# A mixture-of-experts layer whose first twelve expert tiles run off a list made before attention has ended

## The chip, the cores and the metric

The kernel runs on one core of a Trainium2 chip, as one launch. The metric is the device time in microseconds (us), the median of three runs. TensorE (PE in the profile) does matmuls, VectorE (DVE), ScalarE (ACT) and GpSimd (POOL) work on tiles in SBUF and PSUM, SyncE (SP) issues DMAs, and GpSimd issues those with indices (indirect DMAs).

## The reference

Eight sequences of 512 tokens with 512 features pass through cross-attention (16 heads) and a mixture of experts, each with a layer norm ahead and a residual around it. All is float32.

```python
x = x + attention(layernorm(x), ctx, ctx)          # B=8, S=512, D=512, 16 heads of 32
flat = layernorm(x).reshape(4096, 512)
scores = softmax(flat @ router_weight.T + router_bias)   # E=8 experts
topk_vals, topk_idx = top_k(scores, 2)
w = zeros.at[arange[:, None], topk_idx].set(topk_vals)
gu = einsum('th,ehf->tef', flat, gate_up_proj) + gate_up_bias
gate = minimum(gu[..., :512], 7.0); up = clip(gu[..., 512:], -7.0, 7.0)
act = (up + 1.0) * gate * sigmoid(gate * 1.702)
down = einsum('tei,eih->teh', act, down_proj) + down_bias
x = x + einsum('teh,te->th', down, w)
```

## The kernel before

It has three stages, each a block of its own: a block's engines meet at its end (a DRAIN on each, and an exchange of semaphores) before the next block begins. Lines 1129, 1363 and 1799 are the ends of attention_stage, routing_stage and expert_stage.

**Attention** runs over 32 units (a batch b and a chunk c of four heads). The function step(s) lists what is done while unit s takes its exponentials, in eight rounds; all engines walk the one list ORDER and do their own part of it. A unit's output projection, residual, second layer norm and router logits follow some steps later, a tile of 128 tokens at a time (keys "norm", "out", "x2", "rstd", "ln2", "turn_xln", "logits", "logit_sum", "logit_out"). x2 and the normed rows (xln_dram) go to memory. Routing goes along by groups of tiles (route_groups): "best" finds the two experts of each token, "count" keeps running counts, "rank" gives each token its place within its expert by two matmuls, "place" makes the positions, and "list" writes token numbers by indirect DMAs of GpSimd into token_list, which has 32 rows of 128 places for each expert. "soft" and "share" make the weights of the two experts. The last group has five tiles.

**Routing** (routing_stage) makes the counts into whole tiles of 256 tokens for each expert: 39 tiles, with tile_expert, tile_changed (does the tile need other weights than the tile two before), tile_hot and token_of (the token of each place). The last group's tokens are put in by matmuls of one-hot rows (at_hot, col_hot), the others by reading token_list back.

**Experts** (expert_stage) runs over the 39 tiles. in_list takes even tiles from the first half of the list and odd ones from the second, so there are two sets of weights in SBUF, and each is loaded only if the expert changed. All products are in three passes of a high and a low part (fp32r), so that a weight needs, after its DMA into raw_g or raw_d, wg_hi or wd_hi (ScalarE) and wg_lo or wd_lo (VectorE, gate_up_lo and down_lo). For a tile i TensorE transposes the gathered rows (turn_rows), does gate/up in four parts f (96 matmuls of 256 columns, L1489) and down (24 of 512 columns, L1503); it works in the order turn_rows(i+2), gate_up(i+1), down(i). VectorE does in each part: clip (L1612, L1614), glu (L1619, L1622), hidden_lo (L1627), between them xgT_lo of the next rows (row_lo), the pieces of the next weights, and at f = 1 the mix (L1645, L1648), which adds the down result of tile i-1 to the gathered sums. down(i) waits for that mix, since d_ps has one bank for each half. GpSimd gathers rows (L1733) and sums (L1745) and scatters sums (L1750); SyncE loads weights and biases behind two register loads each.

```python
load_if_changed(e, tile_expert, tile_changed, tile, semaphore, experts, copies)   # SyncE: two value_loads, a conditional DMA
with e.If_ne(changed, 0):
    gu_lo(e, s, k)
with e.Else():
    e.sem_inc(wg_lo_made[s], 1)
```

Of the kernel before, what the change touches and what calls it, by code (L numbers as in the profile page):

```python
# [14 lines left out]
P = 128  # L15
# [8 lines left out]
PASSES = ((0, 0), (0, 1), (1, 0))  # L24

# [12 lines left out]
def list_tile(e, token_list, listed, pos, token, n):  # L38

    places = token_list.rearrange("r (q a) -> (r q) a", a=1)  # L40
    for s in range(TOP_K):
        at = bass.IndirectOffsetOnAxis(ap=pos[:, s, n:n + 1].bitcast(U32), axis=0)
        e.indirect_dma_start(out=places, out_offset=at, in_=token[:, n:n + 1], in_offset=None).then_inc(listed, 16)
# [25 lines left out]
def attention_stage(nc, x, ctx_t, w_t, bq, bk, bv, bo, router_wt, router_b, out, xln_dram, w_rows, w_stored, token_list, listed, stored, route, ident):  # L69
# [9 lines left out]
    expo, hots, weight, exp_sum, inv_sum = (route[n] for n in ("expo", "hots", "weight", "exp_sum", "inv_sum"))  # L79

    SLOTS = 2 * T
    GROUPS = route_groups(B * T, T)
    groups = range(len(GROUPS))
    tiles_of = lambda g: slice(GROUPS[g][0], sum(GROUPS[g]))
    slots_of = lambda g: slice(GROUPS[g][0] % SLOTS, GROUPS[g][0] % SLOTS + GROUPS[g][1])

    with ExitStack() as ctx:
# [4 lines left out]
        def begin_at(name, place):  # L92

            gap = (place - nc.sbuf_base) % 128
            if gap:
                ctx.enter_context(nc.sbuf_tensor(f"gap_{name}", [P, gap], mybir.dt.uint8))
# [8 lines left out]
        begin_at("weights", 0)  # L105
        for n in "kv":
# [3 lines left out]
        ctxT, ctx_raw = split("ctxT", [P, C, S])  # L110
        wo = sb("wo", [P, C, D])
        xT = sb("xT", [P, C, S])
# [6 lines left out]
        hi, lo = ({n: sb(f"{n}_{part}", [P, S], F32R) for n in "kq"} for part in ("hi", "lo"))  # L119
        qs = [sb(f"qs{i}", [P, GROUP, S], F32R) for i in range(RING)]  # L120
        ks = [sb(f"ks{i}", [P, GROUP, S], F32R) for i in range(RING)]
# [23 lines left out]
        consts_i = sb("consts_i", [P, route["consts"].shape[1]], I32)  # L145
        tri = sb("tri", [P, P], BF16)
        expert_less = sb("expert_less", [P, E])
        logits = sb("logits", [P, SLOTS, E])
        masked = sb("masked", [P, SLOTS, E])
        best = sb("best", [P, TOP_K, SLOTS])  # L150
        pick = sb("pick", [P, SLOTS])
        pos = sb("pos", [P, TOP_K, GROUPS[-1][0]], I32)
        pos_f = sb("pos_f", [P, TOP_K, SLOTS])

# [19 lines left out]
        def step(s):  # L174
# [49 lines left out]
            for r, lag, *keys in ((1, 9, ("best", 0)), (2, 9, ("best", 1)), (3, 9, ("count",)), (5, 9, ("soft",)),  # L224
                                  (2, 10, ("rank",)), (3, 10, ("place",)), (1, 11, ("share",))):
                g, odd = divmod(s - lag, T)
                if g in groups[:-2] and not odd:
                    at(r, *[(kind, g, *what) for kind, *what in keys])
            g, t = divmod(s - 11, T)
            if g in groups[:-3]:  # L230
                at(3, ("list", g, t))
            if s == units[-1]:
                at(2, ("list", groups[-3], 0))
                at(3, ("list", groups[-3], 1))
            if s == units[-1] + 1:
                at(1, ("list", groups[-3], 2), ("list", groups[-3], 3))
# [27 lines left out]
            if s + 2 in units:  # L264
# [28 lines left out]
                else:  # L293
# [4 lines left out]
                    at(4, ("low", u, "q"), ("v", u, 0))  # L298
# [1606 lines left out]
```

## Time and profile before

| | |
|---|---|
| median of three runs | 1712.31 us (1709.18 to 1713.91) |
| the profiled execution | 1708.13 us |
| its span in the profile | 1706.4 us |
| mean granted TensorE clock | 0.974 |
| TensorE busy | 1588.7 us, 93% of the span |
| VectorE busy | 1268.3 us, 74% |
| ScalarE, GpSimd busy | 656.5 us, 839.8 us |

A window's row gives for each engine the busy microseconds and, in brackets, the instructions. A timeline's row is start, length, engine, line, operation, output and inputs with shapes, how many were merged, and in square brackets the idle time before it with what ended it. In the chain a row is start, length, engine, result and line.

### The profile page before, as it was taken

The page shows a single profiled execution, that of the slowest core. Times are in us where ns is not written, and L with a number is a line of the kernel's source. Part 1 is how long each engine was busy: PE and PEld are TensorE (multiplying, and loading weights), DVE is VectorE, ACT ScalarE, POOL GpSimd, SP SyncE. Part 2 cuts the span into 40 slices and gives each one's busy share as a digit, 9 for nine tenths or more (in the row PEclk, how much of TensorE's full clock was granted, in tenths as well). Part 3 has the DMA queues.
Part 4 walks back from the last instruction along what each step waited for, and adds up shares of the span by engine and source line. Part 5 has one row for each costly group of instructions (what it writes and reads, how often), then busy time and mean ns, then how long its engine had stood idle before and what let it go on. Part 6 is the DMA issues. An engine that isn't in the chain of part 4 may idle for free. (4 is left out here: it accounts for less than half of the span.)

```text
span 1706.4 us, 30244 instructions
## 1 busy us (share of the span) xinstructions
PE 1588.7 (93%) x9612; PEld 1164.9 (68%) x9612; DVE 1268.3 (74%) x2414; ACT 656.5 (38%) x1267; POOL 839.8 (49%) x634
## 2 busy tenths in 40 slices
PE   6898999999999999999998379999999999999995
PEld 4555555565555555655543179999999998999994
DVE  4576777878768778787685668777888788777873
ACT  3254544545445445454443143223333234223320
POOL 3355656566566676666677322333343333333332
PEclk9899999999999999999999779999999999999997
DMA  6343333443443434433321262325443353324321
GB/s 219 82 113 85 107 107 92 120 99 92 108 104 103 103 97 109 109 89 105 102 80 33 65 218 65 99 88 174 162 165 110 97 210 118 107 82 155 107 88 62
DMA packets 101125, 188.99 MB, mean 111 GB/s; under 512 B 28192, under 2 KB 29600, under 8 KB 100960
## 3 DMA queue, kind: packets, MB, share of 16 engines
q1 hardware_dynamic: 79936, 124.25, 26.0%
q0 software_dynamic: 20832, 62.49, 11.6%
q8 instruction: 77, 1.26, 0.4%
q14 instruction: 88, 0.72, 0.2%
q10 hardware_dynamic: 192, 0.26, 0.0%
HBM read 204.32 MB, written 37.51 MB: 142 GB/s over the span
## 5 line engine op out<-in xcount | busy, mean ns | idle before, releaser
L805 DVE TENSOR_REDUCE negmax<-max_ps 128x2 f32<-128x1024 f32 x252 | 306.9, 1218 | 159.3 <-PE max_ps L545 158.5
L674 ACT ACTIVATE pt<-work 128x512 f32<-128x512 f32 x512 | 278.4, 595 | 275.8 <-PE work L557 265.0
L986 POOL TENSOR_TENSOR acc<-acc,pt 128x1024 f32<-128x1024 f32 x128 | 303.4, 2373 | 127.8 <-ACT pt L674 127.7
L1489 PE MATMUL gu_ps<-xgT_hi,wg_hi 128*128 128x256 f32 x1248 | 349.8, 280 | 1.5 <-DVE xgT_lo L1604 1.5
L1489 PE MATMUL gu_ps<-xgT_lo,wg_hi 128*128 128x256 f32 x1248 | 346.4, 278 | 0.0
L1489 PE MATMUL gu_ps<-xgT_hi,wg_lo 128*128 128x256 f32 x1248 | 346.3, 277 | 0.0
L983 POOL TENSOR_TENSOR acc<-pt 128x1024 f32<-128x1024 f32 x64 | 153.3, 2397 | 184.6 <-PE work L577 115.3
L1489 PEld LDWEIGHTS gu_ps<-xgT_hi,wg_hi 128*128 128x128 f32 x1248 | 235.6, 189 | 2.0 <-issue 1.9
L1750 POOL DMA_INDIRECT out<-acc,token_of x78 | 77.0, 987 | 324.6 <-DVE acc L1648 318.6
L1489 PEld LDWEIGHTS gu_ps<-xgT_lo,wg_hi 128*128 128x128 f32 x1248 | 235.8, 189 | 0.1
L1489 PEld LDWEIGHTS gu_ps<-xgT_hi,wg_lo 128*128 128x128 f32 x1248 | 235.5, 189 | 0.0
L545 PE MATMUL max_ps<-ks,qs 96*128 96x512 f32 x504 | 194.2, 467 | 23.4 <-DVE negmax L805 12.9
L1559 ACT ACTIVATE sig<-gate 128x256 f32<-128x256 f32 x156 | 65.1, 418 | 320.4 <-DVE gate L1612 320.4
L557 PE MATMUL work<-qs,ks 98*128 98x512 f32 x512 | 172.2, 413 | 11.0 <-DVE q_lo L792 5.3
L557 PEld LDWEIGHTS work<-qs,ks 98*128 98x128 f32 x512 | 94.5, 190 | 67.6 <-issue 32.0
L545 PEld LDWEIGHTS max_ps<-ks,qs 96*128 96x128 f32 x504 | 85.6, 193 | 78.4 <-issue 50.1
L569 PE MATMUL o_ps<-pt,v 128*32 128x512 f32 x1024 | 136.4, 605 | 2.0 <-ACT pt L674 2.0
L1503 PE MATMUL d_ps<-wd_hi,hid_hi 128*128 128x512 f32 x312 | 124.2, 398 | 10.1 <-DVE acc L1645 9.6
L1745 POOL DMA_INDIRECT acc<-out,token_of x78 | 80.7, 1035 | 103.6 <-DMA out<-acc,token_of 91.2
L507 PE MATMUL work<-xT,wq 128*128 128x512 f32 x256 | 125.0, 611 | 0.9 <-DMA wq<-wq_t 0.9
L1503 PE MATMUL d_ps<-wd_lo,hid_hi 128*128 128x512 f32 x312 | 124.6, 399 | 0.0
L1503 PE MATMUL d_ps<-wd_hi,hid_lo 128*128 128x512 f32 x312 | 124.0, 397 | 0.0
(221 smaller groups left out, 2897.9 us busy)
## 6 DMA issues: line engine op xcount, KB each, us to landing
raw_g<-w_gate_up SPq DMA_DIRECT2D x39, 2048.0 KB
raw_d<-w_down SPq DMA_DIRECT2D x39, 1024.0 KB
qs<-q_hi SPq DMA_DIRECT2D x252, 64.0 KB, 2.0
ks<-k_hi SPq DMA_DIRECT2D x252, 64.0 KB
bd<-b_down SPq DMA_DIRECT2D x39, 256.0 KB
x_in<-x SPq DMA_DIRECT2D x36, 256.0 KB, 3.3
ctxT_raw<-ctx_t SPq DMA_DIRECT2D x32, 256.0 KB, 4.1
xln_dram<-x SPq DMA_DIRECT2D x32, 256.0 KB, 2.3
```

What stands on the lines that cost most here:

```text
L507: ins = e.matmul(to[:, :], wq[:, k, cols], xT[:, k, :], start=(k == 0), stop=(k == C - 1))
L545: ins = e.matmul(pair_of(u, r)[:, j, :], qs[i][0:3 * HD, h, t * P:(t + 1) * P], ks[i][0:3 * HD, h, :], start=True, stop=True)
L557: e.matmul(to[:, :], ks[i][0:3 * HD + 2, h, k * P:(k + 1) * P], qs[i][0:3 * HD + 2, h, :], start=True, stop=True).then_inc(exp_ready.sem, 1)
L569: ins = e.matmul(o_ps[u % 2][HD * h:HD * (h + 1), :], v[:, k, c * P + HD * h:c * P + HD * (h + 1)], pt[k % 2][:, h, :], start=(k == 0), st ...
L674: e.activation(pt[k % 2][:, h, :], in_work("exp", u, k, h)[:, :], ACT.Exp, scale=scale).then_inc(exped.sem, 1)
L805: e.tensor_reduce(negmax[:, u % 2, n:n + 2], pair_of(u, r)[:, :, :], AX.X, ALU.max, negate=True).then_inc(maxed.sem, 1)
L983: e.tensor_tensor(acc[:, heads, :], pt[0][:, heads, :], pt[1][:, heads, :], ALU.add).then_inc(added.sem, 1)
L986: e.tensor_tensor(acc[:, heads, :], acc[:, heads, :], pt[k % 2][:, heads, :], ALU.add).then_inc(added.sem, 1)
L1489: ins = e.matmul(gu_ps[n % GU_BANKS][:, part, :], wg[s][pw][:, k, cols], xgT[s][px][:, k, :], start=(k == 0 and m == 0), stop=(k == KD - 1 ...
L1503: ins = e.matmul(d_ps[j][:, :], hid[s][px][:, k, j * P:(j + 1) * P], wd[s][pw][:, k, :], start=(k == 0 and m == 0), stop=(k == KF - 1 and ...
L1745: e.indirect_dma_start(out=acc[s][:, j, :], out_offset=None, in_=out_rows, in_offset=slot_rows(i, j)).then_inc(acc_in[s], 16)
L1750: e.indirect_dma_start(out=out_rows, out_offset=slot_rows(i, j), in_=acc[i % 2][:, j, :], in_offset=None).then_inc(scattered.sem, 16)
```

## The change

The list of tiles is cut in two. An early list has twelve tiles of 256 places, all of them full, from the tokens of the first five batches; it is made in attention's steps 27 and 28 from the counts so far (whole_tiles, whole_rows), and at steps 31 and 32 SyncE reads the token numbers back (12 loads), loads the first weights, ScalarE and VectorE split tile 0's gate/up weights, and GpSimd gathers the rows of tiles 0 and 1. These buffers stand where attention's weights, context and stacks of keys were. The routing stage as a block is gone. The rest of the tokens go into a main list of 27 tiles. Its routing, for a last group that now has eight tiles, is done within tiles 0 to 10 of the experts: VectorE takes one step of a generator (route) behind each part f, TensorE does its matmuls in tiles 2, 7, 8 and 9. The mix of tile i-1 moves from f = 1 to the head of the tile's loop, ScalarE's down_hi moves behind f = 1. raw_d and wd_lo share a place, so load_down waits for the down matmuls that used it. In attention the low part of q is placed ahead of the norms of round 4. Places in SBUF are set anew so that operands begin at chosen offsets.

```diff
+EARLY = 12
+EARLY_STEPS = (2, 7, 8, 9)
-    return [(n, batch) for n in range(0, last, batch)] + [(last, batch - 1), (last + batch - 1, batch + 1)]
+    return [(n, batch) for n in range(0, last, batch)] + [(last, 2 * batch)]
...
+            if s == EARLY_END + 7:
+                at(2, ("whole_count",))
+                at(3, ("whole_tiles",))
+            if s == EARLY_END + 8:
+                at(3, ("whole_rows",))
+            if s == units[-1]:
+                at(2, ("load_early", "g"), ("whole_tokens",), ("load_early", "d"))
+                at(7, *[("split_early", k) for k in range(C)])
+            if s == units[-1] + 1:
+                at(0, ("load_early", "g1"))
+                at(1, ("token_of",))
+                at(2, ("fetch_early", 0), ("fetch_early", 1))
...
-            g = groups[-2]
-            if s == units[-1] + 1:
-                at(1, ("best", g, 0), ("best", g, 1), ("count", g), ("rank", g))
-                at(2, ("place", g), ("soft", g))
-            if s == units[-1] + 2:
-                at(0, *[("list", g, t) for t in range(GROUPS[g][1])])
-                at(1, ("share", g))
-                at(5, *[(kind, g + 1, *what) for kind, *what in (("best", 0), ("best", 1), ("count",), ("soft",), ("rank",), ("place",))])
+            if s + 2 in units and s >= 0 and c != 2:
+                at(4, ("low", s + 2, "q"))
...
+                    e.wait_ge(rows_made, 1)
+                    e.wait_ge(early["listed"], 16 * TOP_K * EARLY_END)
+                    for i in range(K):
+                        row = e.value_load(early["row"][0:1, i:i + 1], min_val=0, max_val=E * NT - FTOK // P)
+                        e.dma_start(token_in[:, i, :], token_list[bass.ds(row, FTOK // P), :].rearrange("r q -> q r"),
+                                    allow_slow_non_contiguous=True).then_inc(tokens_in, 16)
...
+                elif kind == "fetch_early":
+                    i, = what
+                    if i == 0:
+                        e.wait_ge(early["tokens_made"], 1)
+                        e.wait_ge(w_stored, 16 * (EARLY_G + 1))
+                        for t in range(T):
+                            e.wait_ge(xln_stored[t].sem, xln_stored[t][EARLY_END // T - 1])
+                        e.wait_ge(exp_ready.sem, exp_ready[units[-1], T - 1, GROUP - 1])
+                    fetch_rows(e, early["xg"][i], early["rows"], early["token_of"], in_list(i, K), early["gathered"][i])
...
-def routing_stage(nc, route, stored, w_rows, ...):
...
+            def rank_last():
+                e.wait_ge(before_made, 1)
+                e.matmul(rank_ps, tri[:, :], hots[:, 0:LEFT, :].rearrange("p t e -> p (t e)"), start=True, stop=False)
+                e.matmul(rank_ps, ones_b[:, :], before[:, 0:LEFT, :].rearrange("p t e -> p (t e)"), start=False, stop=True)
+                e.matmul(count_ps, ones_b[:, :], before[:, LEFT, :], start=True, stop=True).then_inc(handed.sem, 1)
+
+            def choose_rows():
+                e.wait_ge(hot_made, TOP_K)
+                late = [(s, t) for s in range(TOP_K) for t in range(LEFT)]
+                for s, t in late:
+                    e.matmul(late_ps, at_hot[:, s, t, :], col_hot[:, s, t, :, :].rearrange("p a n -> p (a n)"), start=((s, t) == late[0]), stop=((s, t) == late[-1]))
...
-                    gate_up(i + 1, range(KF))
+                    gate_up(i + 1, range(KF // 2))
+                    if i + 1 in (LIST_AT, FIRST_AT, RUN_AT):
+                        e.wait_ge(xgT_lo_made.sem, xgT_lo_made[i + 2, 0])
+                    if i + 1 == LIST_AT:
+                        choose_rows()
+                    if i + 1 == FIRST_AT:
+                        send_first()
+                    if i + 1 == RUN_AT:
+                        count_run()
+                    gate_up(i + 1, range(KF // 2, KF))
+                    if i + 1 == RANK_AT:
+                        e.wait_ge(xgT_lo_made.sem, xgT_lo_made[i + 2, 0])
+                        rank_last()
...
-                    down_hi(i + 1, changed_flag(e, i + 1))
...
+                if now == RANK_AT:
+                    soften()
                 for f in range(KF):
                     gate_sigmoid(now, f)
                     if f:
                         hidden_hi(now, f - 1)
+                    if f == 1 and now:
+                        down_hi(now, changed_flag(e, now))
...
+                for s in range(TOP_K):
+                    last()
+                    then(e.tensor_tensor(at_hot[:, s, :, :], iota[:, :].unsqueeze(1).to_broadcast([P, LEFT, P]),
+                                         at_f[:, s, :].unsqueeze(2).to_broadcast([P, LEFT, P]), ALU.is_equal))
+                    yield
...
+            chain = {(0, 0): (best_experts(0), best_experts(1), count_experts()), (RANK_AT, 2): (share(), place_tokens(), main_tiles()),
+                     (LIST_AT, 2): (take_list(),), (FIRST_AT, 2): (take_first(),), (RUN_AT, 2): (take_run(),)}
+            def route(now, f):
+                under_way.extend(chain.get((now, f), ()))
+                if under_way and next(under_way[0], "end") == "end":
+                    under_way.pop(0)
+                    if under_way:
+                        next(under_way[0])
...
+                if i >= 1:
+                    mix(i - 1)
...
-                    if f == 1 and i >= 1:
-                        mix(i - 1)
+                    route(now, f)
+                    if now == RANK_AT - 1 or f == KF - 1 and RANK_AT <= now < LIST_AT:
+                        route(now, None)
...
+                if i == K:
+                    e.wait_ge(tokens_known, 1)
...
+            def load_down(i):
+                s = i % 2
+                if i >= 2:
+                    e.wait_ge(down_made.sem, down_made[i - 2, SUB - 1])
```

## Rows read from the trace of the kernel before

**Rows 1.** Windows: attention, and its end with routing (PE, PEld, DVE, ACT, POOL, PEclk, DMA).

```profile
0.00:905.00 905.00, 854.77 (x4385) 501.20 (x4386) 673.90 (x1062) 420.99 (x778) 564.04 (x363) 0.99 0.40 106
...
961.00:1000.10 39.10, 8.66 (x38) 7.60 (x39) 23.11 (x85) 6.17 (x9) 9.05 (x11) 0.51 0.41 137
```

**Rows 2.** The chain that ended last, from the first gather on.

```profile
996.66 1.98 PE t_ps L1473 x8
...
1000.13 5.46 PE gu_ps L1489 x24
...
1154.53 10.90 PE gu_ps L1489 x96
...
1380.29 5.47 PE gu_ps L1489 x48
...
1437.29 10.89 PE gu_ps L1489 x96
```

**Rows 3.** TensorE's waits, from 1000 us on, then from 60 to 905 us.

```profile
PE d_ps L1503 <- DVE acc L1645: 9.6, 7, 2.8
...
PE work L557 <- DVE q_lo L792: 5.3, 7, 1.0
```

**Rows 4.** Instructions of the block ends L1129 and L1363; DMA from 966 to 974 us.

```profile
L1129 POOLq DRAIN  x1: 18283/18283/18283, 954.8 to 954.8; - x1
...
L1363 POOLq DRAIN  x1: 462/462/462, 973.4 to 973.4; - x1
...
DMA packets 0, 0.00 MB, mean 0 GB/s; under 512 B 0, under 2 KB 0, under 8 KB 0
```

**Rows 5.** Timelines of VectorE, then GpSimd, from 934 to 966 us.

```profile
934.70 2.33 DVE L857 TENSOR_TENSOR ranks<-ranks,expert_less 128x24 f32<-128x24 f32 x1
...
960.75 0.17 DVE L784 TENSOR_TENSOR logits<-work,rb_rows 128x8 f32<-128x8 f32 x1 [1.03 <-PE work L475]
...
965.18 0.20 DVE L900 COPY ranks<-work 128x40 f32<-128x40 f32 x1 [0.41 <-PE work L483]
...
934.63 2.35 POOL L986 TENSOR_TENSOR acc<-acc,pt 128x1024 f32<-128x1024 f32 x1 [5.78 <-ACT pt L674]
...
937.97 1.04 POOL L43 DMA_INDIRECT token_list<-consts,pos  x1 [0.20 <-issue]
...
962.09 0.96 POOL L43 DMA_INDIRECT token_list<-consts,pos  x1 [0.31 <-issue]
```

**Rows 6.** SyncE's timeline: two DMAs, each behind two register loads.

```profile
994.52 0.37 SPq L1376 DMA_DIRECT2D raw_g<-w_gate_up  x1
996.35 0.37 SPq L1376 DMA_DIRECT2D raw_d<-w_down  x1
```

**Rows 7.** VectorE's timeline: the first clip of tiles 0, 1, 2 and 3.

```profile
1007.55 0.48 DVE L1612 TENSOR_SCALAR gate<-gu_ps,bg 128x256 f32<-128x256 f32 x1
...
1023.96 0.48 DVE L1612 TENSOR_SCALAR gate<-gu_ps,bg 128x256 f32<-128x256 f32 x1
...
1038.58 0.48 DVE L1612 TENSOR_SCALAR gate<-gu_ps,bg 128x256 f32<-128x256 f32 x1
...
1053.99 0.48 DVE L1612 TENSOR_SCALAR gate<-gu_ps,bg 128x256 f32<-128x256 f32 x1
```

**Rows 8.** VectorE's timeline: d_lo, a wait for hid_hi, a tile's end without and with weights.

```profile
1030.55 1.28 DVE L1457 TENSOR_TENSOR wd_lo<-raw_d,wd_hi 128x512 fp32r<-128x512 f32 x2
...
1048.30 0.42 DVE L1627 TENSOR_TENSOR hid_lo<-up,hid_hi 128x256 fp32r<-128x256 f32 x1 [0.55 <-ACT hid_hi L1565]
...
1381.58 0.17 DVE L1698 TENSOR_SCALAR bu<-bg 128x4 f32<-128x4 f32 x1 [1.59 <-ACTq L1544]
...
1417.58 2.36 DVE L1454 TENSOR_TENSOR wg_lo<-raw_g,wg_hi 128x1024 fp32r<-128x1024 f32 x2 [1.09 <-ACT wg_hi L1448]
```

**Rows 9.** VectorE's groups by line in the routing stage (busy us, mean ns).

```profile
L1273 DVE TENSOR_TENSOR at_hot<-iota_f,at_f 128x640 f32<-128x640 f32 x2 | 1.6, 822 | 0.0
L1278 DVE TENSOR_TENSOR col_hot<-col_hot,consts 128x390 f32<-128x390 f32 x2 | 1.1, 566 | 0.1
```

More of the change, by code:

```diff
@@ L79, in attention_stage @@
     expo, hots, weight, exp_sum, inv_sum = (route[n] for n in ("expo", "hots", "weight", "exp_sum", "inv_sum"))
+    logits, masked, best, pick, expert_less, tri = (route[n] for n in ("logits", "masked", "best", "pick", "expert_less", "tri"))
     SLOTS = 2 * T
-    GROUPS = route_groups(B * T, T)
+    GROUPS = route_groups(B * T, T)[:-1]
     groups = range(len(GROUPS))
+    EARLY_G = groups[-2]
+    EARLY_END = sum(GROUPS[EARLY_G])
+    K = early["tiles"]
+    NT = B * T
     tiles_of = lambda g: slice(GROUPS[g][0], sum(GROUPS[g]))
@@ L105, in attention_stage @@
         begin_at("weights", 0)
+        first_place = nc.sbuf_base
         for n in "kv":
@@ L1384, in load_down, with place_of @@
[L1384 to L1389 removed]
+def place_of(n_tiles, early, i):
+    K = early["tiles"]
+    return in_list(i, K) if i < K else in_list(i - K, n_tiles - K)
@@ L1399, in expert_stage @@
     tiles = range(n_tiles)
+    K = early["tiles"]
+    MAIN = n_tiles - K
+    SLOTS = MAIN * SUB
+    NT = rows.shape[0] // P
+    LAST = route_groups(NT, batch)[-1]
+    LEFT = LAST[1]
+    weights_stored = len(route_groups(NT, batch))
+    TILE_SHIFT, SHIFT, NUMBER_SHIFT = FTOK.bit_length() - 1, P.bit_length() - 1, 6
     with ExitStack() as ctx:
@@ new lines, in expert_stage @@
+        row_tile = sb("row_tile", [P, MAIN])
+        row_slot = sb("row_slot", [P, SLOTS])
+        choose = sb("choose", [P, E * NT // P, SLOTS])
+        token_1 = sb("token_1", [P, SLOTS])
+        token_f = sb("token_f", [P, SLOTS])
+        pad = sb("pad", [P, SLOTS])
+        first = sb("first", [P, SLOTS])
+        empty = sb("empty", [P, MAIN])
+        spare = sb("spare", [P, MAIN])
+        in_run = sb("in_run", [P, MAIN], BF16)
+        ones_row = sb("ones_row", [1, P])
+        flat_ps = [t_ps[half][:, :, :].rearrange("p a b -> p (a b)") for half in range(KD // 2)]
@@ L1432, in expert_stage @@
+        rows_in, choose_made, token_1_made, run_wanted = (sem(n) for n in ("list_rows_in", "choose_made", "token_1_made", "run_wanted"))
+        experts_known, tokens_known = sem("experts_known"), sem("tokens_known")
+        HANDED = ("rank", "list", "first", "run")
+        handed, taken = Mark(sem("late_handed"), HANDED), Mark(sem("late_taken"), HANDED)
         acc_in = [sem(f"acc_in{s}") for s in range(2)]
@@ L1469, in turn_rows @@
                         e.wait_ge(xgT_lo_made.sem, xgT_lo_made[i - 1, half])
+                    for at_tile, what in zip(EARLY_STEPS, HANDED):
+                        if half == 0 and i == at_tile + 2:
+                            e.wait_ge(taken.sem, taken[what])
                     for k in range(2):
@@ new lines, in count_experts @@
+            def count_experts():
+                last()
+                then(e.tensor_tensor(hots[:, :, :], hot[0][:, :, :], hot[1][:, :, :], ALU.add))
+                then(e.tensor_copy(before[:, 0, :], before[:, LEFT, :]))
+                for t in range(LEFT):
+                    last()
+                    ins = e.tensor_tensor(before[:, t + 1, :], before[:, t, :], hots[:, t, :], ALU.add)
+                    if t + 1 < LEFT:
+                        then(ins)
+                    if t % 4 == 3:
+                        yield
+                ins.then_inc(before_made, 1)
+                e.wait_ge(consts_made, 1)
+                then(e.tensor_copy(iota[:, :], iota_i[:, :]))
+                yield
@@ new lines, in take_list @@
+            def take_list():
+                e.wait_ge(handed.sem, handed["list"])
+                then(e.tensor_copy(token_1[:, :], list_ps))
+                last()
+                then(e.scalar_tensor_tensor(out=token_1[:, :], in0=late_ps[:, 0:SLOTS], scalar=float(1 << NUMBER_SHIFT), in1=token_1[:, :],
+                                            op0=ALU.mult, op1=ALU.add))
+                last()
+                e.tensor_tensor(token_1[:, :], token_1[:, :], late_ps[:, SLOTS:], ALU.add).then_inc(taken.sem, 1)
+                e.wait_ge(taken.sem, taken["list"])
+                e.tensor_scalar(pad[:, :], token_1[:, :], 0.5, None, ALU.is_lt).then_inc(token_1_made, 1)
+                yield
```

770 lines of the change are left out of this document (463 added, 307 removed).

## The prediction

> **What bounds the kernel now.** I read the stage windows first [rows 1]. Up to 905 us TensorE is busy 94% of the time in attention. From 961 to 1000.1 us it works 8.7 of 39.1 us: this is the end of attention's block, the routing stage and the first gathers. Then the chain of waits [rows 2] shows the experts as TensorE's chain: gate/up of tile 0 starts at 1000.13, gate/up of tile 9 at 1154.53. A quiet tile takes 17.27 us (10.90 gate/up, 5.50 down, 0.87 transposes, back to back), so this stage is TensorE bound. It loses time only where weights change: 57.0 us from 1380.29 to 1437.29 for three tiles of 17.27, which is 5.2 lost; all TensorE's waits on the sums (L1645) add up to 9.6 us [rows 3]. I count 7.1 us of stalls behind tile 9 (5.2 for the pair at tiles 24 and 25, the rest at four single changes); the other 2.5 lie in the tail.
>
> Who holds the gap [rows 4, 5]: the last router logits are out at 960.9, VectorE's last attention instruction ends at 965.4, yet the next block waits for GpSimd's DRAIN, which lasts from 954.8 for 18.3 us, to 973.1. GpSimd's last indirect DMA ends at 963.05, so that drain ended 10 us after it. At the next join, without such DMAs before it, the drain took 0.46 us.
>
> **What the change removes.** (1) The routing stage between the blocks, and the four gathers in front of tile 0, leave the path. Attention's tail loses the last group's best/count/rank (960.9 to 965.4), 0.6 us of share and list work. I let the last logits come at 960.3 and the join at 960.7: GpSimd's last indirect DMAs are now the four early gathers. Their price is 1.3 us each (the list DMAs' pitch); behind the lists of 937.97 to 942.9 [rows 5] they end at 948.2, and 10 us of drain end at 958.2, before the join is wanted. The least a drain took is 0.46; counted 10 us from the last piece of GpSimd work (955.5) it would end at 965.5: bounds 0 and +5, taken 0. The early weights are split already, so from the join it is as from 996.66 to 1000.13 [rows 2], 3.5 us: gate/up of tile 0 at G = 964.3 instead of 1000.13, a gain of 35.8.
>
> (2) In attention, q_lo moves ahead of a norm; TensorE waited 5.3 us on it in all [rows 3]. It may return 0 to 5 and cost the norms as much; with some 25 added small VectorE operations at steps 27 and 28 (0.2 us each [rows 5], beside a TensorE that sets the pace) I take -1, bounds -4 and +4.
>
> (3) SyncE gets 12 dynamic loads of the list and three of weights at step 31. I take 1.5 us each, from a pitch of 1.8 where two register loads go with a DMA [rows 6]. From about 911 they end near 932 and land by 935. The tokens are wanted at 943 by GpSimd: hidden, with 8 us to spare. Splitting tile 0's weights (about 4 x 1.2 us) falls where VectorE waited for TensorE between 920 and 933: hidden. If that cover went, a microsecond is a microsecond of the tail.
>
> **What it adds: VectorE's load in tiles 0 to 8.** Here the gain is partly given back. Where VectorE and not TensorE set the pace, the starts of clip for f = 0 in tiles 0 to 3 [rows 7] are 16.4, 14.6 and 15.4 us apart. The 14.6 holds a d_lo of 2.4 (two halves of 1.28, less overlap [rows 8]) and no mix. So a tile without weights has 12.2, plus waits for hid_hi that d_lo had covered (0.55 and 0.2 [rows 8]), plus a mix of 3.0: 15.9. Spare against TensorE's 17.27 is only 1.3.
>
> A weight change adds three pieces on VectorE [rows 8]: at the end of tile c-2 1.8 (idle 1.09 plus 2.36 in place of 1.59), in tile c-1 2.3, in tile c 2.4 for d_lo. The expert order follows from the inputs: the reference's router on them gives the first five batches 4, 2, 2, 1, 3, 2, 1, 2 whole tiles for the eight experts. The twelve first are experts 0,0,0,0,1,1,2,2,3,4,4,4; taken from both halves of the list in turn they change at tiles 0, 1, 5, 7, 8. The main list changes at 12, 13, 17, 18, 24, 25, 30, 34, 38. That is 14 in place of 8 (0, 1, 11, 14, 17, 24, 25, 34).
>
> The late routing is now some 110 VectorE operations in the slots behind the gates. I price them from the routing rows: 0.2 to 0.25 for small ones [rows 5], at_hot for 8 tiles in place of 5 at 0.82 x 8/5, less fixed cost, 1.2 (twice), six col_hot operations of 0.6 (0.57 for 390 elements, now 432) [rows 9]. By tile 0 to 8 this is 2.0, 3.1, 1.3, 2.6, 5.4, 4.2, 0.9, 0.8, 1.0, 21.3 in all; up to 1.2 of a tile's slots fall into the waits for hid_hi and come off. Tile times on VectorE, routing plus pieces of changes (5, 7, 8):
> tile 0: 16.4 + 2.0 = 18.5; 1: 14.6 + 3.1 - 0.5 = 17.2; 2: 16.5; 3: 15.9 + 2.6 - 1.2 + 1.8 = 19.1; 4: 15.9 + 5.4 - 1.2 + 2.3 = 22.4; 5: 15.9 + 4.2 + 2.4 + 1.8 - 1.2 = 23.1; 6: 20.4; 7: 20.2; 8: 18.6. The sum is 176.0. Its first clip is at G + 5.1 (ScalarE has d_hi, then two wg_hi, then two wg_lo follow), so clip of tile 9 is at G + 181.1.
>
> TensorE may run some 8 us ahead, until wg_lo or the gate banks fail it. But at tiles 7, 8 and 9 the code makes it wait, in the middle of gate/up, for xgT_lo of the tile after, made at f = 0 of the same tile, with no slack at all. So TensorE is put back to VectorE's pace there: middle of gate/up of tile 9 at about G + 183, its start counted back at G + 178. Before it was at 1154.53 - 1000.13 = 154.4. Loss: 23.6. TensorE's own new matmuls (3 + 18 + 2 small ones, about 3.5 us) lie inside that wait. ScalarE's Exp for the late group, with two table loads, has 6 us of VectorE's lag to hide in.
>
> **Behind tile 9** mixes come first, which puts the sums 8 to 10 us ahead of their use instead of 2.1, so a pair's excess (about 5) fits: the 7.1 us of stalls go. The weights of the last tile change: d_lo half 1 stands before the last mix, +1.2.
>
> **Sum** on the profiled execution: -35.8 - 1.0 + 23.6 - 7.1 + 1.2 = -19.1, span 1706.4 to 1687.3. Its time was 1708.1, the median 1712.3; on the median -19.1 gives 1693.
>
> **Skill against trace.** The stretch from 966 to 974 has no DMA packet at all, none of instructions either [rows 4], and ends with GpSimd's drain. The Trainium skill, "Runtime: NRT & Kernel Launch", section "Instruction fetch mechanics", says that a taken branch out of the fetched window costs a DMA fetch before execution goes on. By that rule the 8 us would belong to the jump and stay at the one join left, 8 more than in my sum. The trace speaks for the drain.
>
> **Rivals.**
> A, the forecast, 0.52.
> B, the lag is not paid: the steps fill waits, and the stops at tiles 7 to 9 find VectorE in time. Then only 3.5 us of matmuls remain of the 23.6: 1673. For it: VectorE is busy 13 of 17.27 us in quiet tiles. Against: the 15.4 us of its own pace [rows 7]. Anything between B and A is as good as B: 0.17.
> C, the join keeps its 8 us, whatever makes them (the early gathers' drain counted from GpSimd's last work, or the jump): 1701. For it: nobody shows what a drain waits for. 0.12.
> D, tokens of the early list land late (4-byte elements, twelve loads): the fetches stand ahead of the last rstd on GpSimd. From 943 on each microsecond costs one; at 957 all but 5 of the forecast gain is gone, 1707. 0.08.
> E, slower: VectorE's routing operations meet GpSimd's descriptor work. A 24-element multiply took 2.33 us instead of 0.2 while a GpSimd addition ran [rows 5]. Six indirect DMAs of 1 us a tile, each holding VectorE once, are 6 x 9 = 54 us: 1747. It decides for slower from 24 us, 2.7 a tile. Against: clips beside such DMAs keep 0.48 [rows 7]. 0.11.
> The Trainium skill, "SBUF — State Buffer", section "Who interferes with whom": an exclusive lock between VectorE with two SBUF inputs and a GpSimd instruction that reads SBUF. The 2.33 agrees. By the same rule a GpSimd instruction that only writes SBUF leaves such a multiply alone, and if descriptor work is one, E does not come; no row here shows which.
>
> **Range and chances.** 0.3% is 5.1 us, about what this measurement can tell. A's own range is 1685 to 1701 (each tile's pace +-0.5, attention, drain). C and part of B and D widen it to 1677 to 1706. Faster than 1707.2: A, B, C and half of D, 0.84; same 0.06; slower 0.10.
>
> **What would show it.** A drain that ends by 961 and gate/up from about 964; clip starts in tiles 3 to 7 some 19 to 23 us apart; a stop of TensorE in the middle of gate/up at tile 7 on xgT_lo; no wait on acc behind tile 12. I am wrong if the tail waits for tokens, if the drain holds the join, or if clip starts stay near 17.

## The result and the profile after

The changed kernel took 1679.56 us (median of 6 runs, 1677.62 to 1687.31). The kernel before, on the same chip, took 1711.61 (6 runs, 1707.36 to 1713.95). The ratio is 0.983, with a 95% interval of 0.981 to 0.985. The profiled execution of after has a span of 1678.5 us, against 1706.4: 27.9 less, 4.1 less than the 32.0 between the medians. The changed kernel was measured twice more (E1 and E9 below), each time beside the kernel before: 25.8 and 24.0 us between the medians, ratios 0.9845 and 0.9869. So the gain is 24 to 32 us, and the account that follows is of one pair of executions.

I split the span at two events: the end of the last router logits on TensorE, and the first gate/up product of tile 0 (called G below).

| part | before | after | difference | predicted |
|---|---|---|---|---|
| start to the last logits | 960.7 | 952.4 | -8.3 | -1.0 |
| last logits to G | 39.4 | 4.0 | -35.4 | -35.8 |
| G to gate/up of tile 9 | 154.4 | 180.7 | +26.3 | +23.6 |
| gate/up of tile 9 to the end | 551.9 | 541.4 | -10.5 | -5.9 |
| span | 1706.4 | 1678.5 | -27.9 | -19.1 |

The same windows as [rows 1], now up to 895, the rest of attention, and the new gap (PE, PEld, DVE, ACT, POOL, PEclk, DMA share, GB/s):

```profile
0.00:895.00 895.00, 849.36 (x4387) 498.73 (x4388) 681.26 (x1084) 420.08 (x778) 564.91 (x364) 0.99 0.42 107
895.00:952.70 57.70, 47.38 (x204) 21.04 (x202) 30.84 (x58) 19.12 (x36) 35.35 (x33) 0.81 0.76 166
952.70:956.36 3.66, 1.95 (x9) 1.60 (x9) 1.50 (x4) 2.07 (x4) 2.35 (x4) 0.50 0.24 64
```

The 39.1 us in which TensorE worked 8.7 [rows 1] have become 3.66. The chain of waits in that place, which answers to [rows 2]:

```profile
952.91 1.10 PE t_ps L1476 x4
...
954.03 0.60 ACT xgT_hi L1574
...
954.66 0.70 DVE xgT_lo L1652
...
956.36 3.75 PE gu_ps L1492 x16
```

and further on, where tile 9 starts and where the list's last product stands in it:

```profile
1137.08 5.46 PE gu_ps L1492 x48
1142.54 0.70 issue
1143.24 0.19 PE t_ps L1520
1143.42 5.75 PE gu_ps L1492 x48
```

TensorE's waits from 1000 us on, against [rows 3]:

```profile
PE t_ps L1506 <- DVE xgT_lo L1652: 9.8, 1, 9.8
PE d_ps L1532 <- DVE acc L1695: 8.4, 2, 4.3
PE t_ps L1498 <- issue: 2.0, 1, 2.0
PE t_ps L1476 <- DVE padded L1799: 1.2, 1, 1.2
```

One stop of 9.8 us stands in the middle of tile 7's gate/up, at 1093.5, before the routing product of L1506. It is the place where most of VectorE's lag is paid, though not all of it: from one tile's first gate/up product to the next, TensorE takes 22.56, 24.24 and 30.83 us at tiles 2, 6 and 7, where before took 17.57, 17.26 and 17.27. The waits on the sums are two: 4.0 us before the down projection of tile 5, which stands in that step of tile 6, and 4.3 in the last tile. Behind the 4.0 and behind the 9.8 the granted clock is 0.50 (1.2 GHz) for 4 us. Behind tile 9 every tile takes 17.27 us until the tail.

The last instructions of attention's block, against [rows 4]:

```profile
L1293 POOLq DRAIN  x1: 8519/8519/8519, 942.8 to 942.8; - x1
...
L1293 DVEq DRAIN  x1: 205/205/205, 952.4 to 952.4; - x1
```

GpSimd's drain ends at 951.3 and VectorE's begins at 952.4: VectorE comes last, and the join costs half a microsecond. VectorE's timeline, the first clip of tiles 0 to 3, against [rows 7]:

```profile
961.73 0.48 DVE L1660 TENSOR_SCALAR gate<-gu_ps,bg 128x256 f32<-128x256 f32 x1 [0.64 <-PE gu_ps L1492]
...
981.49 0.48 DVE L1660 TENSOR_SCALAR gate<-gu_ps,bg 128x256 f32<-128x256 f32 x1
...
1000.78 0.48 DVE L1660 TENSOR_SCALAR gate<-gu_ps,bg 128x256 f32<-128x256 f32 x1
...
1017.25 0.48 DVE L1660 TENSOR_SCALAR gate<-gu_ps,bg 128x256 f32<-128x256 f32 x1
```

### The profile page after: what moved, and what is told of

It is laid out like the page before. It is cut to its first block and busy times, and to the rows that moved or that the text cites. A ratio compares the mean times of both kernels' runs of the same rounds, so it can differ in the third digit from the quotient of the medians.

```text
span 1678.5 us, 30420 instructions
## 1 busy us (share of the span) xinstructions
PE 1587.3 (95%) x9607; PEld 1165.3 (69%) x9607; DVE 1309.5 (78%) x2477; ACT 694.2 (41%) x1316; POOL 836.8 (50%) x628
## 5 line engine op out<-in xcount | busy, mean ns | idle before, releaser
L1492 PE MATMUL gu_ps<-xgT_hi,early_wg_hi 128*128 128x256 f32 x640 | 179.8, 281 | 1.5 <-DVE xgT_lo L1652 1.5
L1492 PE MATMUL gu_ps<-xgT_lo,early_wg_hi 128*128 128x256 f32 x640 | 177.9, 278 | 0.0
L1492 PE MATMUL gu_ps<-xgT_hi,early_wg_lo 128*128 128x256 f32 x640 | 177.7, 278 | 0.0
L1492 PE MATMUL gu_ps<-xgT_hi,wg_hi 128*128 128x256 f32 x608 | 170.6, 281 | 0.0
L1492 PE MATMUL gu_ps<-xgT_lo,wg_hi 128*128 128x256 f32 x608 | 168.7, 278 | 0.0
L1492 PE MATMUL gu_ps<-xgT_hi,wg_lo 128*128 128x256 f32 x608 | 168.6, 277 | 0.0
L2025 POOL DMA_INDIRECT out<-acc,token_of x54 | 54.1, 1001 | 182.6 <-DVE acc L1698 174.6
L1492 PEld LDWEIGHTS gu_ps<-xgT_hi,early_wg_hi 128*128 128x128 f32 x640 | 121.3, 189 | 2.0 <-issue 1.9
L1492 PEld LDWEIGHTS gu_ps<-xgT_lo,early_wg_hi 128*128 128x128 f32 x640 | 121.4, 190 | 0.1
```

The lines of the kernel that those rows point to most:

```text
L1492: ins = e.matmul(gu_ps[n % GU_BANKS][:, part, :], wg[s][pw][:, k, cols], xgT[s][px][:, k, :], start=(k == 0 and m == 0), stop=(k == KD - 1 ...
L2025: e.indirect_dma_start(out=sums_of[i], out_offset=rows_at[i][j], in_=acc[i % 2][:, j, :], in_offset=None).then_inc(scattered.sem, 16)
```

## The experiments

Attention's length turned out to differ by up to 7 us between executions of the same attention code (last logits at 948.8 in E5, at 955.6 in E11), which is more than most of these edits are worth. So each profile is read in pieces. In the table, "units" is the time between the 10th and the 32nd turn of the maxima on TensorE (L551 before, L605 after), "gap" is last logits to G, "tile 9" and "end" are counted from G. All starts are those of TensorE's timeline, which for tile 9 lie 0.2 under those of the chain. In each of the three sets (before and after; E1 to E4, E5 to E8, E9 to E12) the kernel before ran too.

| kernel | units | gap | tile 9 | end | median | before's median |
|---|---|---|---|---|---|---|
| before | 615.4 | 39.4 | 154.2 | 706.3 | 1711.6 | |
| after | 606.1 | 4.0 | 180.5 | 722.1 | 1679.6 | 1711.6 |
| E1 after again | 608.0 | 5.1 | 180.9 | 722.1 | 1681.1 | 1706.9 |
| E2 q_lo back | 611.9 | 4.0 | 178.9 | 720.7 | 1686.4 | 1706.9 |
| E3 before, q_lo ahead | 607.2 | 39.9 | 155.3 | 707.3 | 1699.6 | 1706.9 |
| E4 mix back | 606.9 | 4.5 | 177.5 | 735.1 | 1696.9 | 1706.9 |
| E5 steps behind | 606.2 | 4.0 | 177.1 | 718.4 | 1679.1 | 1704.6 |
| E6 at_hot thrice | 606.4 | 4.0 | 184.9 | 727.0 | 1682.6 | 1704.6 |
| E7 gathers last | 605.9 | 7.4 | 181.1 | 722.8 | 1684.2 | 1704.6 |
| E8 d_lo on GpSimd | 607.6 | 4.5 | 180.8 | 729.4 | 1689.7 | 1704.6 |
| E9 after, third time | 608.3 | 4.0 | 179.3 | 720.5 | 1684.0 | 1708.0 |
| E10 steps behind again | 609.4 | 4.8 | 177.1 | 718.5 | 1676.2 | 1708.0 |
| E11 mixes ahead | 607.9 | 4.0 | 177.9 | 719.5 | 1678.6 | 1708.0 |
| E12 both | 609.5 | 3.4 | 175.2 | 717.3 | 1675.5 | 1708.0 |

Five profiles leave the expert stage unedited (after, E1, E2, E7, E9): their "end" is 720.5 to 722.8, mean 721.7. That mean is the yardstick for the stage.

**E1: the changed kernel again.**

> The changed kernel once more, nothing edited: the yardstick for the others of this call, and a second profile. Theory: 1680, the first gate/up of tile 0 at 956 to 957 and the wait of the first routing product in tile 7 near 10 us, as in the first profile. What is open is whether TensorE's granted clock of 0.50 to 0.63 between 935 and 960 belongs to the kernel or to that one execution: if it belongs to the kernel it is there again and the last logits come 23 us behind the last sums; if not, they come 19 to 20 behind, and tile 0 starts some 3 us earlier.

Ratio to before 0.9845 (0.9828 to 0.9861). The stage repeats to 0.1 us (E2 and E9 show that this was luck). The granted clock of 0.50 at attention's end is not here: it is 1.00 from 925 to 953. But it did not belong to one execution either. Over the last 18 us ahead of the last logits it is 1.00 in E1, E10 and E12, as in before and E3, and 0.59 to 0.89 in the other nine profiles of the changed program. What lowers it was not tried. Yet G, at 958.9, is not earlier, since this execution was already 3.2 us behind at the last turn of the maxima, and the gap is 1.1 longer: GpSimd's drain ends at 955.1, behind the last logits at 953.8.

**E2: q_lo back behind the norms.**

```
-            if s + 2 in units and s >= 0 and c != 2:
-                at(4, ("low", s + 2, "q"))
...
-                    at(4, ("v", u, 0))
+                    at(4, ("low", u, "q"), ("v", u, 0))
```

> The changed kernel with the subtraction that makes q_lo back behind the normalisation in attention's rounds. Unit by unit the changed kernel's attention ran 10 us ahead of the one before by unit 31: steps of 1.0 to 1.3 at six units, and one of 4.2 at unit 17. Theory (the order does it): the six steps return, 6 to 7 us, so about 1686.5, and TensorE's waits on q_lo (7 of them before, 5.3 us) are in the trace again. Rival (the places of the operands do it): no change, 1680, and no waits. The 4.2 us at unit 17 belong to neither if they don't return.

TensorE's waits from 60 to 905 us in this kernel:

```profile
PE max_ps L597 <- DVE negmax L870: 13.4, 21, 0.8
PE work L609 <- DVE q_lo L857: 5.4, 7, 1.0
```

The seven waits are back, 5.4 us of them; in after the view has none. The median is 5.3 above E1's.

**E3: that one edit in the kernel before.**

```
+            if s + 2 in units and s >= 0 and c != 2:
+                at(4, ("low", s + 2, "q"))
...
-                    at(4, ("low", u, "q"), ("v", u, 0))
+                    at(4, ("v", u, 0))
```

> The kernel before with that one edit of attention's order, operands' places untouched. Theory (order): 6 to 7 us faster than before, about 1705. Rival (places): 1711.5, as before. The stop of 2.85 us at 463 followed by a granted clock of 0.80 in the kernel before: if it belonged to that one execution, it is absent here and the profile is shorter by 4 us more than the medians are.

7.3 under the median of before, with the operands' places untouched; the ratio, 0.9965 (0.9946 to 0.9983), allows 3 to 9 us. The order did it, from both sides, and the places did nothing that these runs show. The waits from 60 to 900 us:

```profile
PE max_ps L547 <- issue: 2.5, 1, 2.5
```

This is the stop that before has at 463 us. I had set it down to one execution; it is here again, but behind it the granted clock stays at 1.00, where in before it fell to 0.59.

**E4: the mix back behind the second clip.**

```
-                if i >= 1:
-                    mix(i - 1)
...
+                    if f == 1 and i >= 1:
+                        mix(i - 1)
```

> The changed kernel with the mix of tile i-1 back behind the second clip of tile i+1, where the kernel before had it; the down projection's high parts stay where the change put them. Theory (the mix's place is what took the stalls behind tile 9 away): TensorE waits on acc again before the second down of each pair with changed weights, 8 to 10 us in all behind tile 9, so 1688 to 1690. Rival (the stalls had gone because VectorE's list order of gates and weights changed): under 2 us, 1680 to 1682.

More than expected: 15.8 over E1's median, and 13.5 over the yardstick in the stage. TensorE's waits behind 1137 us, here and, in the second fence, in after:

```profile
PE d_ps L1532 <- DVE acc L1695: 13.7, 11, 4.3
```

```profile
PE d_ps L1532 <- DVE acc L1695: 4.3, 1, 4.3
```

Up to tile 9 the edit gains 3 us. From tile 9 to the end it takes 557.7 instead of 541.6, 16 more. Waits make 9.4 of that. Behind the last-but-one stop TensorE's granted clock is 0.77 for 7.5 us, another 1.7. Some 5 us stay open, spread over several tiles of 17.8.

**E5 and E10: the routing products behind the four groups.**

```
+                    gate_up(i + 1, range(KF // 2, KF))
                     if i + 1 in (LIST_AT, FIRST_AT, RUN_AT):
                         e.wait_ge(xgT_lo_made.sem, xgT_lo_made[i + 2, 0])
                     if i + 1 == LIST_AT:
                         choose_rows()
...
-                    gate_up(i + 1, range(KF // 2, KF))
...
-                     (LIST_AT, 2): (take_list(),), (FIRST_AT, 2): (take_first(),), (RUN_AT, 2): (take_run(),)}
+                     (LIST_AT, 3): (take_list(),), (FIRST_AT, 3): (take_first(),), (RUN_AT, 3): (take_run(),)}
```

> The changed kernel with TensorE's routing products of tiles 7, 8 and 9 behind all four gate/up groups of the tile in place of between the second and the third, and VectorE's reading of them one group later. Theory (those products have no slack, and TensorE pays there all that VectorE lags): VectorE gets the time of two more groups, 3.45 us, before TensorE stops for it, the wait in tile 7 falls from 9.8 to about 6.3, and 3 to 3.5 us are gained at the last stop: 1676.5. Rival (the lag is paid anyway, in the next wait, because it is VectorE's work that sets the pace to tile 9): 1680, the wait in tile 7 shorter and those behind it longer by as much.

> The edit of the routing products behind the four groups, again, beside its yardstick. Its first profile had 718.4 us from tile 0 to the end, 3.7 less than the changed kernel, and tile 9 at 177.1, while the medians of different calls didn't show a gain. Theory (a gain of 3.7, hidden by attention's scatter between executions): 718.4 again and a median some 3.5 under the yardstick's. Rival (none): the median within 1 us of it.

In the stage both profiles agree, 718.4 and 718.5: 3.2 under the yardstick, near the 3.45 us of slack put in. The stop in tile 7 fell further than I had said, and part of it came back as waits for the routing's results. TensorE's waits in E10, from 1000 to 1160 us:

```profile
PE t_ps L1506 <- DVE xgT_lo L1652: 4.4, 1, 4.4
PE t_ps L1476 <- DVE padded L1799: 2.7, 1, 2.7
PE d_ps L1532 <- DVE acc L1695: 2.5, 2, 2.0
PE t_ps L1476 <- DVE token L1904: 2.4, 1, 2.4
```

In medians E10 is 7.8 under E9, of which the stage explains some 2 to 3; E5's ratio of 0.9858 (0.9843 to 0.9874) shows no gain over E1's 0.9845. So the stage's gain is measured, the kernel's only in one of two sets.

**E6: more work for VectorE.**

```
+                    for again in range(3):
+                        last()
                         then(e.tensor_tensor(at_hot[:, s, :, :], iota[:, :].unsqueeze(1).to_broadcast([P, LEFT, P]),
                                              at_f[:, s, :].unsqueeze(2).to_broadcast([P, LEFT, P]), ALU.is_equal))
```

> The changed kernel with the comparison that makes at_hot (1.22 us each, one for each of two choices, in tiles 4 and 5) made three times each: 4.9 us more of VectorE, the same output. Theory (VectorE sets the pace up to the stop in tile 7): the stop ends 4.9 later and the whole is 4.9 longer, 1684.5. Rival (VectorE's lag is slack and the stop is a matter of the routing's chain or of ScalarE, for which VectorE idles 7.4 us at the weights' high parts): under 1 us.

Four comparisons more, all of them in VectorE's tile 4 (1033.0 to 1060.0 here), not in tiles 4 and 5; its timeline has them as

```profile
1039.52 3.73 DVE L1852 TENSOR_TENSOR at_hot<-iota_f,late_at_f 128x1024 bf16<-128x1024 f32 x3
...
1049.19 3.73 DVE L1852 TENSOR_TENSOR at_hot<-iota_f,late_at_f 128x1024 bf16<-128x1024 f32 x3
```

which is 3.73 in place of 1.22, 5.0 us in all. The stage is 5.4 over the yardstick (4.9 over after and E1). A microsecond of VectorE there is a microsecond of the stage. The kernel's median can't show it alone: 1682.6 is 1.5 over E1's, and the ratio to before, 0.9890, is 0.2 to 0.6% over those of the changed kernel.

**E7: the early gathers last.**

```
-                at(2, ("fetch_early", 0), ("fetch_early", 1))
+            if s == units[-1] + 2:
+                at(1, ("fetch_early", 0), ("fetch_early", 1))
```

> The changed kernel with the first four gathers of rows issued by GpSimd behind its last instruction of attention, near 943 to 949, in place of 932 to 937. What is tested is GpSimd's drain at attention's end. In the kernel before it ended 10.0 us behind the issue of the last indirect transfer, in the changed kernel 14.4 behind it, hidden there. Theory (it waits out the indirect transfers, 10 us or more): it ends at 959 or later, the join moves from 952.7 to 959, tile 0 starts 6 us later and the whole is 6 longer, 1686. Rival (it needs a time from GpSimd's last instruction of any kind, 7.9 us): it ends at 957, +4. Second rival (the gathers themselves are what tile 0 waits for): they land at 952 and nothing moves, 1680.

```profile
953.41 1.94 PE L1478 MATMUL t_ps<-ident,early_xg 128*128 128x128 f32 x8 [3.91 <-PEq L1295]
```

TensorE waits 3.9 us for the join, against 0.5 in after: the gap is 3.4 longer. GpSimd's drain ends at 953.1, 5.4 behind the end of the last gather's issue at 947.7. So 10 us or more were wrong for gathers, and so was the 7.9. The time from GpSimd's last instruction to the drain's end, in all profiles:

| kernel | last GpSimd instruction ends | which | drain ends | behind it |
|---|---|---|---|---|
| E2, E5, E6, E11, E12 | 953.1, 939.8, 943.3, 946.6, 947.9 | rstd | 958.5, 945.1, 948.6, 951.9, 953.2 | 5.3 |
| E10, E1, E9, E8, E4, after | 945.9 to 948.2, after 943.4 | rstd | 951.3 to 955.5 | 6.3 to 7.9 |
| E7 | 947.7 | gather of rows | 953.1 | 5.4 |
| before, E3 | 963.1, 952.9 | write of the list | 973.1, 963.5 | 10.1, 10.6 |

The last row is of the program before alone, so the write of the list and the rest of that program are not told apart; nor was it tried what makes 5.3 in some profiles and up to 7.9 in others.

**E8: the down weights' low parts on GpSimd.**

```
on_dve:  -                    else:
         -                        down_lo(now, f - 2, down_changed)
on_pool: +                if i + 1 < n_tiles:
         +                    down_lo(i + 1)
```

> The changed kernel with the low parts of the down weights, four subtractions of 0.69 us for each tile with new weights, on GpSimd in place of VectorE. Theory (VectorE's load sets tiles 0 to 8, five of them with new weights): 2.6 us less for each, up to 13 less lag and a gain of some 8 to 12, 1668 to 1672, if the two engines don't hold each other up. Rival (they do: in this trace subtractions of VectorE take up to twice their time beside GpSimd's): GpSimd's four take 1.2 us each or more, VectorE's own grow by about what it was spared, and the time is 1678 to 1682. Second rival: GpSimd's gathers and stores queue behind the subtractions and TensorE waits for rows: slower, above 1684.

Slower, by 7.7 in the stage. One place shows why VectorE gained nothing from being spared. GpSimd's timeline and, in the second fence, VectorE's beside it:

```profile
1070.35 5.40 POOL L1453 TENSOR_TENSOR wd_lo<-raw_d,wd_hi 128x512 fp32r<-128x512 f32 x4 [3.58 <-issue]
```

```profile
1071.25 0.67 DVE L1667 TENSOR_TENSOR gate<-gate,sig 128x256 f32<-128x256 f32 x1
1071.96 1.40 DVE L1670 SCALAR_TENSOR_TENSOR up<-up,gate 128x256 f32<-128x256 f32 x1
1073.28 0.34 DVE L1882 TENSOR_REDUCE row_tile<-step_of 128x27 f32<-128x189 f32 x1
1073.65 0.89 DVE L1884 TENSOR_SCALAR row_tile<-row_tile,early_first 128x27 f32<-128x27 f32 x1
1074.58 1.25 DVE L1887 TENSOR_TENSOR row_slot<-iota_f,row_tile 128x54 f32<-128x54 f32 x1
```

Alone these take 0.42, 0.43, 0.34, 0.24 and 0.22 us: VectorE lost 2.9 us beside four subtractions that it would have made in 2.6. The largest loss is in tile 0, and another stands in the last tile; VectorE's timeline at both, and in the second fence GpSimd's at the last:

```profile
961.52 7.85 DVE L1450 TENSOR_TENSOR wg_lo<-early_raw_g,wg_hi 128x1024 fp32r<-128x1024 f32 x2 [2.15 <-ACT wg_hi L1444]
...
1661.11 4.04 DVE L1667 TENSOR_TENSOR gate<-gate,sig 128x256 f32<-128x256 f32 x1
```

```profile
1659.88 4.99 POOL L1453 TENSOR_TENSOR early_wd_lo<-early_raw_d,wd_hi 128x512 fp32r<-128x512 f32 x4
```

In after they take 2.36 and 0.42 us. Tile 9 starts at 180.8, as if nothing had been moved. The loss of 7 us lies behind: TensorE waits 9.2 us on acc in 7 waits (once 6.2) where after has one of 4.3. The time fits the second rival, but a queue on GpSimd is not what the trace shows there: the mixes come late because VectorE's products ahead of them are held, as the 4.04 ahead of the last mix, for which TensorE then waits 6.2. The Trainium skill, "SBUF — State Buffer", section "Who interferes with whom", has an exclusive lock between a VectorE instruction with two SBUF inputs and a GpSimd instruction that reads SBUF; the 0.67, 1.40 and 1.25 agree, and so do the 7.85 and the 4.04; the 0.89 is of another form, with one tile and a column as inputs.

**E9, E11 and E12: the yardstick, mixes ahead, both edits.**

```
+        LAGGING = range(9)
...
-                if i >= 1:
+                if i >= 1 and i - 1 not in LAGGING:
                     mix(i - 1)
...
+                if i in LAGGING:
+                    mix(i)
                 if i + 3 < n_tiles:
                     changed = changed_flag(e, i + 3)
                     for k in range(KD // 2):
                         gate_up_lo(i + 3, k, changed)
```

> The changed kernel, nothing edited, as the yardstick of this call. The attention stage's length differs by up to 6 us between executions of one kernel, so the stages are read apart: from the first gate/up of tile 0 to the end 722.1 us in both profiles so far. Expected: the same 722 again, gate/up of tile 9 at 180.5 to 181 behind tile 0's, and 0.983 to 0.985 of the kernel before.

> The changed kernel with the mix of tile i, for i from 0 to 8 alone, made at the end of tile i+1 ahead of VectorE's first two low parts of gate/up weights, in place of behind them. At the ends of tiles 0 to 8 VectorE stands idle 12.8 us for ScalarE to reach the high parts of those weights, or to find that they don't change. Theory (that idle time is part of VectorE's lag): the mix fills it, some 1.2 us a tile, and 6 to 9 us are gained at the stop: tile 9 at 172 to 175, 1671 to 1674. Rival (VectorE waits for something else in its place, so the lag stays): the sum of its idle time in tiles 0 to 8 is as large as before, tile 9 at 180.5.

> Both edits: mixes ahead of the splits in tiles 1 to 9, and TensorE's routing products of tiles 7 to 9 behind the four groups. Theory (both shorten what VectorE lags at the last stop, and add up): 3.7 and 6 to 9, so 709 to 713 us from tile 0 to the end, and a median 10 to 13 under the yardstick's, near 1669. Rival (once VectorE lags less, the next wait is ScalarE's or the down projection's): less than the larger of the two alone, 715 or more.

E9 missed its expectation: 720.5 in place of 722, tile 9 at 179.3, ratio 0.9869. So the stage repeats to about 2 us, and gains of 2 are near what one profile can tell. Mixes ahead (E11) gain 2.2 in the stage where I expected 6 to 9, and both together (E12) 4.4 where I expected 9 to 13. The times were nearer the rivals', though E12's rival said less than the larger of the two alone, and the two nearly add up (3.2 and 2.2). VectorE's waits from 956 to 1137 us add up to 20.4 in E11 against 22.4 in E9: most of its idle time didn't go, it moved. E11, VectorE's waits from 956 to 1137 us:

```profile
DVE bu L1971 <- PE gu_ps L1493: 4.5, 3, 1.6
DVE wg_lo L1450 <- ACT wg_hi L1444: 3.9, 2, 2.1
DVE hid_lo L1676 <- ACT hid_hi L1607: 3.1, 10, 0.5
```

The first of these stands before VectorE's first operation of a tile. In E9 that operation is the mix, and the waits before it (acc L1695) are 4.9 us. E12 has the lowest median of the study, 1675.5 (ratio 0.9819, 0.9793 to 0.9846), against E9's 1684.0 (0.9869, 0.9846 to 0.9892); of the 8.5 between them the stage shows 3.2, and the intervals touch. It is a likely gain of some 3 to 4 us over the changed kernel, no more.

## Why the prediction was right, point by point

The time lies in the stated range, 1677 to 1706, but only in the part that C, B and D had widened: 1679.6 is outside A's own 1685 to 1701, and 13 us under the forecast of 1693. The mechanisms of A are what the runs show; the size came out right with luck, since attention's term alone missed by more than its bounds.

**The gap.** Right: from the logits to tile 0 it is 4.0, as forecast (960.3 to 964.3). The 0.4 between -35.8 and -35.4 is the earlier last logits, which the sum had in this term and the table has in attention's, where the forecast is then -1.4. The rival of the join that keeps its 8 us (C, by the drain or by the jump) fell: the drain was over before VectorE was done, and the join costs 0.5 us in after. There the low clock helped to hide the drain: GpSimd's last instruction ended 9.0 us ahead of the last logits, in E1, at a granted clock of 1.00, only 5.6. By the rule of the Trainium skill, "Runtime: NRT & Kernel Launch", section "Instruction fetch mechanics", on a taken branch out of the fetched window, as I had read it, the 8 us would have stayed. In after the trace doesn't agree: TensorE waits 0.5 us there.

**The drain.** The price was wrong, though it stayed hidden. I counted 10 us from the last indirect DMA, 948.2 to 958.2. That DMA ended at 936.9, and the drain at 951.3, 14.4 behind it. Over 14 profiles it comes 5.3 to 7.9 us behind GpSimd's last instruction of whatever kind, except in the two of the program before, where that is a write of the list and it is 10.1 and 10.6. It isn't as far off the path as I had it: in E1 it held the join 1.1 us.

**Attention, -1.0 forecast, -8.3 measured.** This is the largest miss, and outside the bounds of -4 and +4. The units between the 10th and the 32nd turn gave 9.3 and what lies ahead of them 1.0; the end, from the last turn to the last logits, took 1.9 back (56.5 us against 54.6), at the low clock of this execution. The term held back a gain that [rows 3] had in full: 5.3 us of waits on q_lo, which I let come back as waits of the norms. E2 and E3 show that little or nothing came back: 4.4 us longer (611.9 against a mean of 607.4 over the twelve profiles with q_lo ahead), and 7.3 us off the median of before. Most of the rest is one stop. At the same place of the program, the first maxima product behind the 16th turn, TensorE stands still with nothing to wait for, in every profile: 2.85 us in before, 2.5 in E3, 0.2 to 1.5 in the twelve of the new program. In before the granted clock fell to 0.59 over the next 4 us (1.2 GHz for most of them), and the unit was 4.2 longer than in after. That compares two extremes: after has the shortest such unit (26.9 us; 27.0 to 28.2 in the other eleven), and E3, whose clock did not fall, has 29.2 against before's 31.1. So a good part of the 4.2 belongs to these two executions. What makes the stop, and why the old program has more of it, was not tried.

**SyncE's loads and the early split: hidden,** as said. Twelve loads took 15.45 us in place of 18, and the list's tokens were there early. Rival D found no ground.

**VectorE's load, +23.6 forecast, +26.3 measured.** The mechanism is shown: the stop is on xgT_lo in tile 7, E6 gives one for one, E5 and E10 give back what slack they add. Rival B (the lag fills waits) is out. The first clips of tiles 0 to 9 are 19.8, 19.3, 16.5, 19.0, 22.0, 22.5, 19.8, 22.5 and 18.6 apart, 180.0 in all against 176.0. Tiles 2 to 6 are within 0.7 of the forecast. Off were tile 0 (+1.3: VectorE waits 1.7 us for wg_hi at 964.3, which before has not), tile 1 (+2.1: the mix of tile 0 now stands at the head of the loop, so this stretch holds its 3.0 us, and I had built tile 1 on the 14.6 without one) and tile 7 (+2.3: VectorE waits 2.7 us for TensorE's second half behind the stop, which my sum left out).

**Rival E,** the routing's operations beside GpSimd's descriptor work, is out as well: the 156 products of L1667 in after, with 221 indirect DMAs among them, take 409 to 427 ns each, the slowest included. E8 shows what does hold VectorE: GpSimd's arithmetic on SBUF.

**Behind tile 9, -5.9 forecast, -10.5 measured.** From tile 9 to tile 38 it is 501.2 in place of 507.0; with the new product in tile 9 (1.3) taken off, that is the 7.1 us of stalls, gone. The tail I had wrong. It is 4.7 us shorter, not 1.2 longer: its stall before tile 37's down projection (2.5 and 0.5 in before) is gone too, and with it a stretch of 8 us at a granted clock of 0.79. The new weights of the last tile cost about what I said: the last wait is 4.3 in place of 2.8. Some 1.5 us of the tail stay open. E4 shows that the mix's place is what does this, and that it is worth more than the chain of before could tell, 16 us behind tile 9. The changed list has more weight changes for stalls to sit on, and E4's waits stand by them (tiles 12, 17, 24, 29, 37 and 38), but 5 of the 16 us are not explained.

Together: attention gave 7.3 us more than forecast and the tiles behind tile 9 gave 4.6 more, the join 0.4 less and VectorE's load took 2.7 more. That is the 8.8 us between -19.1 and -27.9. The 4.1 us by which the medians are further apart than the two profiled executions are scatter that no piece explains.

## What to carry to other kernels

Here a wait that the view put on one operation in the wrong order was a gain almost in full; I took a fifth of it without a row that showed who would pay for the rest. Test such a term by itself, as E3 does. Where an engine that is not the bottleneck lags, look for the first place at which the bottleneck must meet it without slack: by there the whole lag is paid, and slack put in at that place came off nearly one for one (3.2 of 3.45 us), while filling the laggard's idle time may only move it. When executions of a kernel differ by more than an edit is worth, cut the profile at fixed events and compare the pieces.

## What the runs showed of the hardware

- GpSimd's drain at a block's end lasted 5.3 to 7.9 us beyond its last instruction where that was arithmetic or a gather (the 12 profiles of the changed program), 10.1 and 10.6 where it was a scattered write of 4 bytes (the 2 of the program before); at a second join without indirect DMAs in the block it took 0.46 [rows 4].
- A stop of TensorE can cost more than itself: behind 2.85 us the granted clock was 0.59 over 4 us (before), behind 4.3 us 0.77 over 7.5 us (E4), behind 9.8 us 0.50 over 4 us (after). Behind 2.5 us at the same place of the program it stayed at 1.00 (E3).
- VectorE and GpSimd, both with two operands in SBUF, gained nothing from sharing the work: 2.9 us lost for 2.6 spared at one place, and a VectorE product of 0.42 us took 4.04 while three of GpSimd's subtractions followed on each other (E8). The same subtraction takes GpSimd 1.47 us (median) and VectorE 0.68.
- A VectorE product with both inputs in SBUF kept its time beside GpSimd's indirect DMAs (409 to 427 ns, 156 of them, in after).
